# A routed feed-forward stage: its logits in one batch, and its threshold search at two bits an iteration

## The reference

```
logits = xf @ Wr + br
Sm = softmax(logits, axis=-1)               # [tokens, 8]
G_t, idx_t = top_k(Sm.T, k)                 # k = n_tok // 8, per expert
tokens = xf[idx]
mid = silu(einsum('keh,ehf->kef', tokens, Wu) + bu)
out = einsum('kef,efh->keh', mid, W_down) + b_down
y = zeros_like(xf).at[idx].add(G[..., None] * out)
```

## Time and profile before

| | us |
|---|---|
| median of 3 runs | 8431.38 |
| lowest and highest of them | 8424.31, 8488.79 |
| the profiled execution's own time | 8455.97 |
| its span in the trace | 8454.1 |

### The profile page before, as it was taken

One profiled execution on the slowest core, in us unless ns is written; L12 is line 12 of the kernel. 1 busy time (PEld: TensorE's weight loads), 2 busy tenths in 40 slices (PEclk: granted clock), 3 DMA queues, 4 the chain that ended last, 5 costly groups with the idle time before them and its releaser, 6 DMA issues. The chain is left out here.

```text
span 8454.1 us, 243652 instructions
## 1 busy us (share of the span) xinstructions
PE 6789.6 (80%) x92884; PEld 4792.7 (57%) x92884; DVE 5620.9 (66%) x11929; ACT 4975.8 (59%) x10706; POOL 4197.0 (50%) x3732
## 2 busy tenths in 40 slices
PE   5777999999999999999999599987888577633267
PEld 2325666666666666666666488885555323323245
DVE  6895776777677677677677377766667488735332
ACT  4545777777777777777777344436767554302122
POOL 4555665666566566566666245554444355430000
PEclk8888999999999999999999699998999788866578
DMA  3221111111111111111111200000000132321001
GB/s 126 120 98 52 40 41 50 40 38 49 42 41 49 41 38 48 42 41 46 43 41 39 74 5 5 6 13 22 15 23 16 39 146 108 149 68 52 21 0 30
DMA packets 234165, 413.24 MB, mean 49 GB/s; under 512 B 41944, under 2 KB 125360, under 8 KB 214128
## 3 DMA queue, kind: packets, MB, share of 16 engines
q1 hardware_dynamic: 225344, 377.76, 14.2%
q10 hardware_dynamic: 1584, 15.21, 0.4%
q0 software_dynamic: 6144, 5.25, 0.4%
HBM read 208.61 MB, written 32.18 MB: 28 GB/s over the span
## 5 line engine op out<-in xcount | busy, mean ns | idle before, releaser
L763 POOL TENSOR_TENSOR L0f_qr<-L0f_qs,L0f_table 128x512 f32<-128x512 f32 x776 | 989.2, 1275 | 461.9 <-ACT L0f_qs L804 358.9
L1018 PE MATMUL L0f_ring<-L0f_wqkv,L0f_hT 128*128 128x512 f32 x2324 | 1173.3, 611 | 42.2 <-ACT L0f_hT L799 37.5
L770 POOL TENSOR_TENSOR L0f_qr<-L0f_qr,L0f_m 128x512 f32<-128x512 f32 x776 | 984.9, 1269 | 162.2 <-issue 106.5
L834 ACT ACTIVATE L0f_scores<-L0f_scores,L0f_nmx,L0f_rn 128x64 f32<-128x64 f32 x3072 | 982.5, 400 | 132.0 <-DVE L0f_nmx L939 130.8
L1075 PEld LDWEIGHTS L0f_o<-L0f_pT,L0f_vmix 64*64 64x64 f32 x18480 | 759.1, 137 | 158.7 <-issue 136.0
L1075 PE MATMUL L0f_o<-L0f_pT,L0f_vmix 64*64 64x32 f32 x18480 | 801.4, 221 | 50.6 <-ACT L0f_pT L842 31.8
L1075 PE MATMUL L0f_o<-L0f_pT,L0f_vb 64*64 64x32 f32 x6160 | 750.6, 221 | 0.7 <-issue 0.4
L777 POOL TENSOR_TENSOR L0f_qr<-L0f_qr,L0f_rn 128x512 f32<-128x512 f32 x388 | 396.3, 1042 | 687.7 <-DVE L0f_rn L931 686.4
L908 DVE TENSOR_TENSOR L0f_m<-L0f_ring,L0f_table 128x512 f32<-128x512 f32 x776 | 524.0, 685 | 254.9 <-ACT L0f_qs L804 246.3
L1075 PEld LDWEIGHTS L0f_o<-L0f_pT,L0f_vb 64*64 64x64 f32 x6160 | 604.3, 137 | 2.3 <-issue 2.3
L916 DVE TENSOR_REDUCE L0f_ssq<-L0f_sq 128x8 f32<-128x512 f32 x776 | 509.6, 675 | 76.7 <-ACT L0f_sq L809 71.9
(11 more groups left out here) (538 smaller groups left out, 17117.0 us busy)
## 6 DMA issues: line engine op xcount, KB each, us to landing
L0f_vmix<-L0f_vb SPq DMA_DIRECT2D x768, 128.0 KB, 2.5
L0a_bc_all<-L0a_bc_rows SPq DMA_DIRECT2D x32, 2048.0 KB, 11.4
L2a_bc_all<-L2a_bc_rows SPq DMA_DIRECT2D x32, 2048.0 KB, 11.3
L0f_vmix<-L0f_vb SPq DMA_DIRECT2D x672, 64.0 KB, 2.0
L1f_vmix<-L1f_vb SPq DMA_DIRECT2D x96, 128.0 KB, 2.4
L0f_wqkv<-L_ffn_wqkv_dram SPq DMA_DIRECT2D x7, 1536.0 KB, 6.2
L2f_parts<-L2f_zero ACTq DMA_DIRECT2D x8, 1088.0 KB, 11.4
n_s<-mixer_out SPq DMA_DIRECT2D x32, 256.0 KB, 5.0
```

The costliest lines, as they stand in the source:

```text
L763: e.tensor_tensor(rotated, qs[:, q % QN], spread(cos, 1, 8), ALU.mult).then_inc(cosed.sem, 1)
L770: e.tensor_tensor(rotated, rotated, m2[:, q % SN], ALU.add).then_inc(added.sem, 1)
L834: a = e.activation(s_ps[:, s, h, j], s_ps[:, s, h, j], ACT.Exp, bias=nmx[:, s, col:col + 1], scale=rn[:, tt, 2 * u, col:col + 1])
L1018: e.matmul(bank[:], hT[:, tt * P:tt * P + P], wqkv[:, layer % 2, col:col + 512], start=True, stop=True).then_inc(full, 1)
```

## The change

*Logits.* The loops are written out. PE transposes straight from `g.f` into two PSUM banks in turn; POOL's copy is gone, and so are `fb` and `fbT`: ACT copies each bank once, into `xT`, and the product with `wr` reads that. All 32 tiles' logits go to one PSUM tile of [128, 32, 8], and bias, maximum, subtraction, exponential, sum, inverse and product are done once for all of them. The first sequence's transposes stand ahead of the wait for the loads. There are three more loads: `same` (128x128, one where two partitions have the same expert), `lower` (the same, and only from earlier tiles) and `digits` (128 x 15 x 3 integers).

*Search.* PE transposes `rate` in two halves, so that a partition holds one expert and one tile of each half: 16 tiles by 8 experts on the partitions, 2 x 128 tokens along them (`rT`). The threshold is one value per partition. An iteration fixes two bits: three candidates (`cand`), and for each one comparison of all of `rT` with a scalar of the partition, which also writes its count through the accumulator output (`accum_out`). PE sums the three counts over the partitions of an expert by a product with `same`. DVE compares the three sums with 512 and counts how many reach it, through the accumulator output again; that is the digit, 0 to 3. It is scaled by a power of four and set in `kth`. There are 15 iterations, without a loop. In the tail the equal ones are numbered by scans along the tokens and products with `lower` and `same`; the masked `rT` is transposed back and copied over `rate`.

The diff, with removed lines left out (they stand in the listing above):

```diff
@@ -328,7 +328,13 @@
...
+    p = np.arange(P)
+    same = p[:, None] % 8 == p[None, :] % 8
+    lower = same & (p[:, None] // 8 < p[None, :] // 8)
+    digits = np.arange(1, 4)[None, :] << (2 * np.arange(14, -1, -1))[:, None]
+    return {"same": same.astype(np.float32), "lower": lower.astype(np.float32),
+            "digits": cont(np.broadcast_to(digits, (P,) + digits.shape).astype(np.int32)),
+            "wr": get("Wr"), "br": get("br").reshape(1, -1), "wu": cont(get("W_up").transpose(1, 0, 2)),
...
@@ -3521,6 +3527,7 @@
...
+    DIGITS = 15
...
@@ -3533,166 +3540,160 @@
...
+        same = sb("same", [P, P])
+        lower = sb("lower", [P, P])
+        digits = sb("digits", [P, DIGITS, 3], I32)
...
         with stage(nc, name + "s") as r:
...
+            lg = r.sb("lg", [P, NT, E])
+            mx = r.sb("mx", [P, NT])
+            t_ps = [r.ps(f"t{k}", [P, 512]) for k in range(2)]
+            l_ps = r.ps("l", [P, NT, E])
+            loaded = r.sem("loaded")
+            turned, copied, rated = r.sem("turned"), r.sem("copied"), r.sem("rated")
+            shifted, exped = r.sem("shifted"), r.sem("exped")
             block = r.block()
...
             @block.sync
...
+                for dst, src in ((wu, "wu"), (bu, "bu"), (wd, "wd"), (bd, "bd"), (same, "same"), (lower, "lower"), (digits, "digits")):
...
+                e.wait_ge(loaded, 144)
...
             @block.tensor
...
+                def turn(b):
+                    if b >= 2:
+                        e.wait_ge(copied, b - 1)
...
+                        o = e.transpose(t_ps[b % 2][:, tt * P:tt * P + P], g.f[:, b * TT + tt, :], g.ident[:])
+                    o.then_inc(turned, 1)
+
+                turn(0)
+                e.wait_ge(loaded, 144)
+                for b in range(BATCH):
+                    if b + 1 < BATCH:
+                        turn(b + 1)
+                    e.wait_ge(copied, b + 1)
...
+                        o = e.matmul(l_ps[:, b * TT + tt, :], xT[:, b, tt * P:tt * P + P], wr[:], start=True, stop=True)
+                o.then_inc(rated, 1)
...
             @block.scalar
...
+                for b in range(BATCH):
+                    e.wait_ge(turned, b + 1)
+                    e.activation(xT[:, b], t_ps[b % 2][:], ACT.Copy).then_inc(copied, 1)
+                e.wait_ge(shifted, 1)
+                e.activation(lg[:], lg[:], ACT.Exp).then_inc(exped, 1)
...
             @block.vector
...
+                e.wait_ge(loaded, 144)
+                e.wait_ge(rated, 1)
+                e.tensor_tensor(lg[:], l_ps[:], spread(br[:], 1, NT), ALU.add)
+                e.drain()
+                e.tensor_reduce(mx[:], lg[:], AX.X, ALU.max)
+                e.drain()
+                e.tensor_tensor(lg[:], lg[:], spread(mx[:], 2, E), ALU.subtract)
+                e.drain().then_inc(shifted, 1)
+                e.wait_ge(exped, 1)
+                e.tensor_reduce(mx[:], lg[:], AX.X, ALU.add)
+                e.drain()
+                e.reciprocal(mx[:], mx[:])
+                e.drain()
+                e.tensor_tensor(rate[:], lg[:], spread(mx[:], 2, E), ALU.mult)
+
+
+        with stage(nc, name + "b") as r:
+            HALF = NT // 2
+            rT = r.sb("rT", [P, 2, P])
+            kth = r.sb("kth", [P, 1], I32)
+            cand = r.sb("cand", [P, 3], I32)
+            add = r.sb("add", [P, 1], I32)
+            hit = r.sb("hit", [P, 3, 2, P])
+            cnt = r.sb("cnt", [P, 3])
+            step = r.sb("step", [P, 3])
+            digit = r.sb("digit", [P, 1])
+            eq = r.sb("eq", [P, 2, P])
+            one = r.sb("one", [P, P])
+            before = r.sb("before", [P, 2, P])
+            room_left = r.sb("room_left", [P, 2])
+            t_ps = r.ps("t", [P, 2, P])
+            n_ps = r.ps("n", [P, 3])
+            g_ps = r.ps("g", [P, 1])
+            b_ps = r.ps("b", [P, 2])
+            turned, counted, summed = r.sem("turned"), r.sem("counted"), r.sem("summed")
+            greater, equal, placed, chosen, back = (r.sem(n) for n in ("greater", "equal", "placed", "chosen", "back"))
+            block = r.block()
+
+            @block.vector
+            def _(e):
+                e.memset(kth[:], 0)
+                e.memset(one[:], 1.0)
+                e.wait_ge(turned, 1)
+                e.tensor_copy(rT[:], t_ps[:])
+                for i in range(DIGITS):
                     e.drain()
...
+                    e.tensor_tensor(cand[:], spread(kth[:, 0], 1, 3), digits[:, i], ALU.bitwise_or)
                     e.drain()
...
+                    for k in range(3):
+                        o = e.tensor_scalar(hit[:, k], rT[:], cand[:, k:k + 1].bitcast(F32), 0.0, ALU.is_ge, ALU.add,
+                                            accum_out=cnt[:, k:k + 1])
+                    e.drain().then_inc(counted, 1)
+                    e.wait_ge(summed, i + 1)
+
+                    e.tensor_scalar(step[:], n_ps[:], KTOK - 0.5, 0.0, ALU.is_ge, ALU.add, accum_out=digit[:])
                     e.drain()
...
+                    e.tensor_scalar(add[:], digit[:], float(4 ** (DIGITS - 1 - i)), None, ALU.mult)
                     e.drain()
...
                 e.drain()
...
+                value = kth[:, 0:1].bitcast(F32)
+                e.tensor_scalar(hit[:, 0], rT[:], value, 0.0, ALU.is_gt, ALU.add, accum_out=cnt[:, 0:1])
+                e.tensor_scalar(eq[:], rT[:], value, None, ALU.is_equal)
                 e.drain().then_inc(greater, 1)
...
+                for h in range(2):
+                    e.tensor_tensor_scan(before[:, h], one[:], eq[:, h], 0.0, ALU.mult, ALU.add)
+                e.drain().then_inc(equal, 1)
+                e.wait_ge(placed, 1)
+
+                e.tensor_scalar(room_left[:], spread(g_ps[:, 0], 1, 2), -1.0, float(KTOK), ALU.mult, ALU.add)
                 e.drain()
...
+                e.tensor_tensor(room_left[:], room_left[:], b_ps[:], ALU.subtract)
                 e.drain()
...
+                for h in range(2):
+                    e.tensor_scalar(before[:, h], before[:, h], room_left[:, h:h + 1], None, ALU.is_le)
                 e.drain()
...
+                e.tensor_tensor(eq[:], eq[:], before[:], ALU.mult)
                 e.drain()
...
+                e.tensor_tensor(hit[:, 0], hit[:, 0], eq[:], ALU.add)
                 e.drain()
...
+                e.tensor_tensor(rT[:], rT[:], hit[:, 0], ALU.mult)
+                e.drain().then_inc(chosen, 1)
+                e.wait_ge(back, 1)
+                e.tensor_copy(rate.rearrange("p (h t) x -> p h (t x)", h=2), t_ps[:])
...
             @block.tensor
...
+                for h in range(2):
+                    o = e.transpose(t_ps[:, h], rate[:, h * HALF:h * HALF + HALF, :].rearrange("p t x -> p (t x)"), g.ident[:])
+                o.then_inc(turned, 1)
+                for i in range(DIGITS):
+                    e.wait_ge(counted, i + 1)
+                    e.matmul(n_ps[:], same[:], cnt[:], start=True, stop=True).then_inc(summed, 1)
...
+                e.matmul(g_ps[:], same[:], cnt[:, 0:1], start=True, stop=True)
+                e.wait_ge(equal, 1)
+                e.matmul(b_ps[:], lower[:], before[:, :, P - 1], start=True, stop=False)
+                e.matmul(b_ps[:, 1:2], same[:], before[:, 0, P - 1:P], start=False, stop=True).then_inc(placed, 1)
+                e.wait_ge(chosen, 1)
+                for h in range(2):
+                    o = e.transpose(t_ps[:, h], rT[:, h], g.ident[:])
+                o.then_inc(back, 1)
...
```

More of the change, by code:

```diff
@@ L3643, in _ @@
                 e.memset(kth[:], 0)
-                e.memset(bit[:], 1 << (BITS - 1))
                 e.memset(one[:], 1.0)
-                e.drain()
-                with e.Fori(0, BITS) as i:
-                    e.tensor_tensor(cand[:], kth[:], bit[:], ALU.bitwise_or)
+                e.wait_ge(turned, 1)
+                e.tensor_copy(rT[:], t_ps[:])
+                for i in range(DIGITS):
                     e.drain()
-                    e.tensor_tensor(hit[:], rate[:], spread(cand.bitcast(F32)[:], 1, NT), ALU.is_ge)
+                    e.tensor_tensor(cand[:], spread(kth[:, 0], 1, 3), digits[:, i], ALU.bitwise_or)
@@ L3684, in _ @@
-                e.drain()
-                e.tensor_tensor(rate[:], rate[:], hit[:], ALU.mult)
+                e.tensor_tensor(rT[:], rT[:], hit[:, 0], ALU.mult)
+                e.drain().then_inc(chosen, 1)
+                e.wait_ge(back, 1)
+                e.tensor_copy(rate.rearrange("p (h t) x -> p h (t x)", h=2), t_ps[:])
             @block.tensor
             def _(e):
-                with e.Fori(0, BITS) as i:
-                    e.wait_ge(*counted(i, "c"))
-                    e.matmul(n_ps[:], g.ones[:], cnt[:], start=True, stop=True).then_inc(summed.sem, 1)
@@ L3692, in _ @@
-                e.wait_ge(greater, 1)
-                e.matmul(n_ps[:], g.ones[:], cnt[:], start=True, stop=True)
-                e.matmul(e_ps[:], g.before[:], eq[:], start=True, stop=True)
```

(3 more changed lines are left out.)

91 lines of the change are left out of this document (removed).

## The result

| | before | changed |
|---|---|---|
| median, us | 8436.85 (4 runs) | 8355.39 (4 runs) |
| lowest, highest | 8424.31, 8488.79 | 8347.21, 8359.98 |
| profiled execution: own time, span | 8455.97, 8454.1 | 8351.0, 8349.2 |

The ratio to the kernel before is 0.9904, with a 95% interval of 0.9888 to 0.9921: the change gains 81 us, between 67 and 94. Measured again beside other kernels the same code gave 0.9917 (0.9904 to 0.9931). The two intervals overlap and cover 58 to 94 us.

A forecast was written before the change was run, and what follows sets the result against it. Serial chains, not a full engine, were taken to bound the logits and search stages. 23.1 - 0.9 + 46.4 + 2.9 = 71.5 us gained, off the median 8431.38: 8360 us, range 8336 to 8396.

The forecast's parts named there:

- loads and logits: Logits stage: PE runs through and one softmax serves all tiles; 23.1 us gained, including loads 0.5 us later.
- entry of the search: Before the first candidate: two transposes of rate and a copy out of PSUM are new; 0.9 us lost.
- search: 15 digits of 3.26 us, 48.9 in all, in place of 30 bits taking 95.3; 46.4 us gained.
- tail: From the search's last OR to the end of the stage: 6.7 us instead of 9.6; 2.9 gained (1 to 4).
- barrier behind it: Between the stages, semaphores cleared and a barrier stay as before and enter the sum with nothing.
- Bound: Logits and search stages: no engine is full, a serial chain bounds each; the expert stage keeps its length.
- The clock: Logits stage: gapless PE work raises the granted clock from 0.50; 6 us more gained, 8354 in all; chance 0.18.
- Double rate: Search comparisons run at double rate: 39 us of search, 81 gained, 8350; chance 0.08, half of it with the clock.
- dear accumulators: Search comparisons run out whole with a costly read-out: 61 us of search, 59 gained, 8372; chance 0.12.
- Late code: DVE between digits waits for straight-line instructions; over 4.8 us a digit removes the gain; chance 0.04 with no shorter search.
- The step without effect: Search not shortened: a digit costs 6.35 us, twice a bit, leaving 25 us gained, 8406; chance 0.04 with late code.
- the likeliest case: Whole kernel: total stays within 1% of the time before; chance 0.74, against 0.23 for faster and 0.03 for slower.

The follow-up runs named there:

- each part alone: New logits stage with the old search: ratio 0.9973 to the kernel before; old logits stage with the new search: 0.9936.
- the kernels with added or wide products: Changed kernel with 32 added 128-column logits products, mixed among narrow ones (logits 46.0 us) or ahead of them (34.4), or with wide products replacing narrow ones (26.4).
- the kernel with wide products alone: Changed kernel with 128-column accumulating logits products in place of 8-column ones, its one wait for all nine loads kept; one execution of 8352.4 us.

## Why the prediction was right

The forecast was 8360 us, the measured median 8355; its gain of 71.5 us stands against 75.4 in the two stages and 81 (67 to 94) in the total. That the medians lie 5 us apart is in part luck: the same kernel gave 8365.61 when it was measured again. What bears the forecast out is the sum inside the stages. Term by term, in the profiled executions:

| term | forecast, us | measured, us | from |
|---|---|---|---|
| loads and logits | +23.1 | +23.3 | 55.64 to 32.34 |
| entry of the search | -0.9 | -0.4 | 1.74 to 2.17 |
| search | +46.4 | +49.8 | 94.68 to 44.93 |
| tail | +2.9 | +2.9 | 9.61 to 6.69 |
| barrier behind it | 0 | -0.2 | 2.16 to 2.32 |

*Bound.* Right: the stages are worth their own chains, since each part alone gave 24.3 and 52.2 us and the sum is the whole to within 1.1. The experts' stage and what follows it kept their length (358.0 us from POOL's first copy to the end of the span before, 358.6 after).

*Logits.* Right, with two small errors that cancel: PE's part was 18.8 us for the 18.5 forecast, and the load came 0.1 us later, not 0.5, which is within its scatter. The softmax took 3.30 us, as forecast.

*Entry of the search.* From the last rate to the first candidate the forecast added 0.9 us, and 0.4 came. The new search does cost 0.8 there (2.17 against the 1.38 with the old search behind the new logits, 2.55 against 1.74 behind the old ones). The other 0.36 are a gain that the prediction put at nothing: the logits stage without loops closes sooner.

*Search.* The mechanism was right, and one term mis-sized: "The accumulator has to be read out, which I price as a small DVE instruction, 0.09". It costs nothing on the path: comparisons start 0.40 apart, not 0.47, and the third reaches PE in 0.57, not 0.64; the step with its own accumulator takes 0.25, not 0.32. With two differences of 0.02 that makes 2.95 in place of 3.26 us a digit, 4.6 us over fifteen. Two late instructions take back 0.74 (44.93 against 44.19 us in the kernels that have none). The forecast's 95.3 and 48.9 us also each hold a way from the last OR to a next candidate, 0.66 and 0.24, that its tail counts once more; measured as in the table, its search was worth 46.0. The single rate, which I chose over the double one, was right, and the kernel without the count shows that the choice was worth 0.42 us a digit, 6.3 in all.

*Rivals.* The clock: the grant stayed at 0.50, so that rival fell for this kernel; its doubt, products of another shape, was the point, as the kernels with added or wide products show. Double rate and dear accumulators fell by the rows of the comparison (475 ns, 0.40 apart; 82 ns beside it). Late code: 0.9 us of idle time in two places against the 4.8 us a digit that it needed; such gaps, taken for one in thirty instructions, came twice in 165. The step without effect: 2.95 us a digit against 6.35.

*The sign and the range.* The measured gain is 0.96% with an interval of 0.79% to 1.12%, and 0.83% (0.69% to 0.96%) again: under the 1% of the likeliest case, with the edge inside the first interval.

## What to carry to other kernels

In a serial search, price a round trip as a fixed part and a part per comparison, and choose the radix where they balance: here 1.75 us and 0.40 us make two bits best of the three widths that ran. Before trimming arithmetic at the head of a stage, ask of each semaphore which of the transfers it counts the next instruction reads: splitting one wait gave 6.4 us in its stage, a quarter of what the whole rewrite of the logits stage gave. A product of few columns is not always the cheap one: here the wide product took 9% more time at 1.2 GHz, and with it the grant went to 2.4 GHz.

## What the runs showed of the hardware that was not expected

- A DVE accumulator read-out (82 ns) starts together with the next comparison and adds no time: 45 comparisons 0.40 us apart.
- PE was busy without a gap for 19 us (32 us with the added products mixed in) at a granted clock of 0.50. With transposes and 128-column products in the same place the grant was 1.00 after 4.2 us, and with 8-column products alone behind them it held for 5.7 us and then fell to 0.50, although PE had no gap.
- At the 1.2 GHz level a product of 8 columns takes nearly the time of one of 128: from a batch's first product to the next transposes are 1.57 us in the changed kernel (7912.70 to 7914.27) and 1.71 in the kernel with wide products alone (7921.31 to 7923.02), four tiles each.
